# A routed feed-forward stage on one core: Gelu moved to PSUM, result sums moved forward

## What is computed

```python
x = x + xattn(layernorm(x), ctx, ...)          # 32 batches x 128 tokens x 128, 16 heads, 77 keys
# the stage that the change touches: 8 experts, the best 2 for each token
n = layernorm(x)
top_v, top_i = top_k(gate_scores(n), 2);  gate_probs = softmax(top_v)
h   = gelu(einsum('bsd,edf->ebsf', n, W1) + b1)   # F = 512
eo  = einsum('ebsf,efd->ebsd', h, W2) + b2
out = x + sum of the two chosen eo, each times its gate_prob
```

## Time and profile before

| | us |
|---|---|
| median of 3 runs | 387.59 (386.9 to 391.44) |
| the profiled execution, its own time | 386.44 |
| its span | 384.7 |
| busy PE, DVE, ACT, POOL | 341.3, 304.0, 291.5, 276.7 |
| mean granted clock of PE | 0.966 |

### The profile page before, as it was taken

How to read it: one execution, slowest core, us unless ns; L and a number is a source line. 1 busy time by engine, 2 the same in 40 slices (tenths; PEclk the granted TensorE clock), 3 DMA queues, 4 the chain that set the end, 5 groups by cost and what they waited for, 6 DMA issues and landing times.

```text
span 384.7 us, 14132 instructions
## 1 busy us (share of the span) xinstructions
PE 341.3 (89%) x3564; PEld 290.9 (76%) x3565; DVE 304.0 (79%) x972; ACT 291.5 (76%) x846; POOL 276.7 (72%) x493
## 2 busy tenths in 40 slices
PE   4799999999999999999997689999999999999800
PEld 3467777777777777777775579999999999999700
DVE  6678999999999999999998647676665666668773
ACT  3799999999999999999986465666566666666621
POOL 5632487777877777777744647888989888789873
PEclk9999999999999999999999869999999999999965
DMA  3132023321333011210000221223222223259156
GB/s 91 44 81 78 23 79 100 100 67 62 97 97 88 33 40 43 85 36 22 23 29 18 64 65 50 65 66 84 73 83 73 69 69 82 56 152 284 33 147 180
DMA packets 42570, 29.19 MB, mean 76 GB/s; under 512 B 5443, under 2 KB 39311, under 8 KB 42528
## 3 DMA queue, kind: packets, MB, share of 16 engines
q1 hardware_dynamic: 34848, 18.60, 18.2%
q0 software_dynamic: 4320, 8.53, 6.6%
q10 hardware_dynamic: 3360, 1.57, 1.4%
HBM read 17.53 MB, written 11.62 MB: 76 GB/s over the span
## 4 chain that ended last, share of the span: by engine, by line
PE 57%; DVE 21%; issue 9%; DMA 4%; ACT 3%; POOL 2%; DVEq 2%; ACTq 0%; SPq 0%; POOLq 0%
PE ps_s L912 15%; PE ps_s L923 13%; PE ps_t L635 7%; PE ps_o L646 4%; PE ps_s L619 4%; DVE sums L1217 3%; DVE mx L1200 3%; PE ps_s L609 3%; DVE rows L1285 2%; PE ps_t L905 2%; PE ps_x L666 1%; DVE pr L1210 1%; DMA ys<-results 1%; PE ps_o L660 1%; DVE x L1239 1%
## 5 line engine op out<-in xcount | busy, mean ns | idle before, releaser
L567 POOL DMA_INDIRECT results<-eo,didx x71 | 70.8, 997 | 22.1 <-POOL didx L556 10.0
L452 POOL DMA_INDIRECT lists<-rows,slots x64 | 66.7, 1043 | 17.7 <-issue 16.9
L912 PE MATMUL ps_s<-xtT,w1c 128*128 128x128 f32 x568 | 78.3, 282 | 1.1 <-DVE xtT L1623 1.0
L923 PE MATMUL ps_s<-w2s,hT 128*128 x568 | 75.8, 277 | 0.2 <-ACT hT L1148 0.2
L963 ACT ACTIVATE pT<-ps_t 77x512 f32<-77x512 f32 x128 | 73.9, 595 | 2.0 <-PE ps_t L635 2.0
L635 PE MATMUL ps_t<-identf,pr 128*77 128x128 f32 x512 | 72.8, 275 | 0.8 <-ACT pT L963 0.7
L912 PEld LDWEIGHTS ps_s<-xtT,w1c 128*128 128x128 f32 x568 | 71.5, 198 | 2.0 <-DVE xtT L1623 1.9
L1144 ACT ACTIVATE w1c<-w1s 128x512 f32 x71 | 44.8, 631 | 35.4 <-PE ps_s L912 34.2
L923 PEld LDWEIGHTS ps_s<-w2s,hT 128*128 128x128 f32 x568 | 69.7, 193 | 0.5 <-issue 0.4
L1637 DVE TENSOR_TENSOR h<-ps_s,b1T 128x512 f32<-128x512 f32 x71 | 49.0, 690 | 25.5 <-PE ps_s L912 23.8
L635 PEld LDWEIGHTS ps_t<-identf,pr 128*77 128x77 f32 x512 | 58.6, 147 | 6.9 <-issue 4.6
(11 more groups left out here) (211 smaller groups left out, 609.3 us busy)
## 6 DMA issues: line engine op xcount, KB each, us to landing
xt<-lists SPq DMA_DIRECT2D x71, 66.0 KB
ys<-results SPq DMA_DIRECT2D x14, 256.0 KB, 3.7
xin<-in_x_dram SPq DMA_DIRECT2D x16, 128.0 KB
w1s<-in_L_ffn_W_dram SPq DMA_DIRECT2D x8, 256.0 KB, 3.2
w2s<-in_L_ffn_W_dram SPq DMA_DIRECT2D x8, 256.0 KB, 3.5
out_dram<-x SPq DMA_DIRECT2D x5, 256.0 KB, 5.6
cin<-in_ctx_dram SPq DMA_DIRECT2D x16, 77.0 KB
results<-eo,didx POOLq DMA_INDIRECT x71
```

What stands on the lines that cost most here:

```text
L452: nc.gpsimd.indirect_dma_start(lists, bass.IndirectOffsetOnAxis(ap=slots[:, r, s * TOPK + k:s * TOPK + k + 1], axis=0), rows[:, r, s, k, : ...
L567: nc.gpsimd.indirect_dma_start(results, bass.IndirectOffsetOnAxis(ap=didx[:, r:r + 1], axis=0), eo[:, r, :], None, bounds_check=TOPK * NTO ...
L912: last = nc.tensor.matmul(ps_s[:, r, c * P:(c + 1) * P], w1c[:, r, c * P:(c + 1) * P], xtT[:, r, :], start=True, stop=True)
L923: last = nc.tensor.matmul(ps_s[:, 2 + r, 0:D], hT[:, r, c * P:(c + 1) * P], w2s[:, bass.ds(e + c * D, D)], start=(c == 0), stop=(c == FC - 1))
```

## The change

- Bias and Gelu become one operation of ACT, straight from PSUM: 4 activations of 128x128, each with the bias column of its 128 features. DVE's `h` goes, and with it the buffer `h`, `h_ready`, `tab_b` and `bias_at`. PE's up product of j+1 now waits for `act_ready` of j-1.
- ACT's step j has another order: Gelu of j first, then the weights of j+2. ACT reads `tab_w` twice in a step.
- 17 batches (`SUMMED`) are summed on DVE beside tiles 60 to 70, one or two for each tile, and 7 more right behind the last tile. POOL and ACT share in the last 8 batches alone. `chances(0, ...)` moves from steps 0 to 2 to step 60.
- SP issues the stores of chunks 0 to 3 before the late loads. Of chunks 6 and 7, SP loads the first results and ACT the second ones. ACT issues the last store.
- POOL's last tile doesn't wait for `pace`, and the last three tiles write none.

```diff
-    EARLY = 11
-    LATER = 3
+    SUMMED = (2, 2, 1, 2, 1, 2, 1, 2, 1, 2, 1)
+    SUMS_FROM = N_TILES - len(SUMMED)
...
-            return b >= EARLY and b % 8 in POOL_OF_8
+            return b >= PART and b % 8 in POOL_OF_8
...
+        def late_results(eng, k):
+            all_returned(eng, N_TILES)
+            for c in range(PART // CH, NB // CH):
                 eng.dma_start(ys[:, c, k, :, :], res[c, k]).then_inc(y_loaded[c], 16)
...
-            all_returned(sp, N_TILES)
-            load_results(sp, PART // CH)
-
-            for c in range(LATER, NB // CH):
+            for c in range(sum(SUMMED) // CH):
+                store(sp, c)
+            late_results(sp, 0)
+            for c in range(sum(SUMMED) // CH, NB // CH - 1):
                 store(sp, c)
...
-                after_tile(pool, FE["paced"], j - 2)
+                if not known(j) or j < N_TILES - 1:
+                    after_tile(pool, FE["paced"], j - 2)
...
-                nc.gpsimd.memset(pace[:, m % 2, :], 0.0).then_inc(FE["paced"], 1)
+                if not known(j) or j < N_TILES - 3:
+                    nc.gpsimd.memset(pace[:, m % 2, :], 0.0).then_inc(FE["paced"], 1)
...
-                    after_tile(pe, FE["h_ready"], j - 1)
+                    after_tile(pe, FE["act_ready"], j - 1)
...
             def tile(j, m):
                 r = m % 2
+                if has(j, 0, N_TILES):
+                    e = act.value_load(tab_w[0:1, j:j + 1] if known(j) else tab_w[0:1, bass.ds(j, 1)],
+                                       min_val=0, max_val=(NE - 1) * F)
+                    after_tile(act, FE["up_done"], j)
+                    after_tile(act, FE["down_done"], j - 2)
+                    settled(act)
+                    for c in range(FC):
+                        last = nc.scalar.activation(hT[:, r, c * P:(c + 1) * P], ps_s[:, r, c * P:(c + 1) * P], ACT.Gelu,
+                                                    bias=b1T[:, bass.ds(e // P + c, 1)])
+                    last.then_inc(FE["act_ready"], 1)
                 if has(j, 2, N_TILES):
...
-                if has(j, 0, N_TILES):
-                    after_tile(act, FE["h_ready"], j)
-                    after_tile(act, FE["down_done"], j - 2)
-                    nc.scalar.activation(hT[:, r, :], h[:, r, :], ACT.Gelu).then_inc(FE["act_ready"], 1)
...
-            act.wait_ge(p_step, 3)
-            for c in range(PART // CH):
-                weigh(c)
-            all_returned(act, N_TILES)
-            for c in range(PART // CH + 1, NB // CH):
-                load_results(act, c)
-            for c in range(LATER):
-                store(act, c)
+            late_results(act, 1)
             act.wait_ge(p_step, 6)
             for c in range(PART // CH, NB // CH):
                 weigh(c)
+            store(act, NB // CH - 1)
...
+            def sum_batches(a, z):
+                if a == 0:
+                    for stage in range(3):
+                        chances(0, stage)
+                    dve.wait_ge(p_step, 3)
+                for b in range(a, z):
+                    if b % CH == 0:
+                        after_y(dve, b // CH)
+                    first_sum(b)
+                for b in range(a, z):
+                    second_sum(b)
...
-                if has(j, 2, N_TILES):
-                    r = m % 2
-                    after_tile(dve, FE["act_ready"], j)
-                    after_tile(dve, FE["up_done"], j + 2)
-                    nc.vector.tensor_tensor(h[:, r, :].rearrange("p (c t) -> p c t", c=FC),
-                                            ps_s[:, r, :].rearrange("p (c t) -> p c t", c=FC),
-                                            b1T[:, bass.ds(e1, FC)].unsqueeze(2).to_broadcast([P, FC, P]), ALU.add
-                                            ).then_inc(FE["h_ready"], 1)
+                if known(j) and SUMS_FROM <= j < N_TILES:
+                    sum_batches(sum(SUMMED[:j - SUMS_FROM]), sum(SUMMED[:j - SUMS_FROM + 1]))
...
-            dve.wait_ge(all_given, 1)
-            second_sum(EARLY - 1)
-            for c in range(EARLY // CH, NB // CH):
-                mine = [b for b in range(c * CH, (c + 1) * CH) if b >= EARLY and not on_pool(b)]
+            sum_batches(sum(SUMMED), PART)
+            for stage in range(3):
+                chances(1, stage)
+            dve.wait_ge(p_step, 6)
+            for c in range(PART // CH, NB // CH):
+                mine = [b for b in range(c * CH, (c + 1) * CH) if not on_pool(b)]
```

More of the change, by code:

```diff
@@ L56, in xattn_moe_kernel @@
     N_ZEROS = 3
-    AHEAD = 3
     AFTER = 3
@@ L64, in xattn_moe_kernel @@
     PTT = 64
-    EARLY = 11
-    LATER = 3
+    SUMMED = (2, 2, 1, 2, 1, 2, 1, 2, 1, 2, 1)
+    SUMS_FROM = N_TILES - len(SUMMED)
     POOL_OF_8 = (2, 5, 7)
-    assert NB % 4 == 0 and PART % 4 == 0 and max(PART_TILES) + AHEAD <= PTT
+    assert NB % 4 == 0 and PART % 4 == 0 and max(PART_TILES) <= PTT
     assert HG * SK <= 512 and HG == 4
-    TT = N_TILES + AHEAD
+    TT = N_TILES
     assert (NE - 1) * FC < 32
@@ L583, in _ @@
             steps(pool, give_back, 0, N_TILES - 1, LOOPED, N_TILES - 2, FRING, between)
-            pool.nop(nofuse=True).then_inc(all_given, 1)
-            for c in range(NB // CH):
+            for c in range(PART // CH, NB // CH):
                 mine = [b for b in range(c * CH, (c + 1) * CH) if on_pool(b)]
@@ L894, in _ @@
             steps(pe, step, 1, 17, 5, 14)
-            pe.wait_ge(tab_ready, 3)
+            pe.wait_ge(tab_ready, 1)
             pe.wait_ge(l_ffn, 16 * FFN_LOADS)
@@ L943, in between @@
                 elif j == LOOPED:
-                    pe.wait_ge(tab_ready, 5)
+                    pe.wait_ge(tab_ready, 2)
             steps(pe, tile, -2, N_TILES, LOOPED, N_TILES - 3, FRING, between)
@@ L1155, in between @@
                 elif j == LOOPED:
-                    act.wait_ge(tab_ready, 5)
+                    act.wait_ge(tab_ready, 2)
             steps(act, tile, -2, N_TILES - 1, LOOPED, N_TILES - 3, FRING, between)
@@ L1451, in table_rows @@
                                         ).then_inc(skip_ready, 1)
[L1452 to L1457, removed]
+                nc.vector.tensor_copy(tab_w[:, a:z], tabs[part][0][0:1, 0:z - a]).then_inc(tab_ready, 1)
             def counted():
@@ L1579, in _ @@
             steps(dve, step, 0, 18, 6, 13)
-            dve.wait_ge(tab_ready, 3)
+            dve.wait_ge(tab_ready, 1)
             dve.wait_ge(wpt_copied, 2)
@@ L1605, in second_sum @@
                                                ALU.mult, ALU.add).then_inc(sum2, 1)
-            def tile(j, m):
[L1608 to L1612, removed]
+            def sum_batches(a, z):
[9 more added lines that the diff above has]
+                    second_sum(b)
+            def tile(j, m):
                 if has(j, -1, N_TILES):
-                    q = (m - 1) % FRING
+                    q, t = (m - 1) % FRING, j - 1
+                    e = dve.value_load(tab_w[0:1, t:t + 1] if known(t) else tab_w[0:1, bass.ds(t, 1)],
+                                       min_val=0, max_val=(NE - 1) * F)
+                    e2 = e // FC
                     after_dma(dve, returned, j - 1 - FRING, q)
@@ L1645, in between @@
                     second_norm(NP - 1, NP - 1)
-                elif 0 <= j < 3:
-                    chances(0, j)
                 elif j == 3:
@@ L1667, in between @@
                 elif j == LOOPED:
-                    dve.wait_ge(tab_ready, 5)
-            steps(dve, tile, -3, N_TILES, LOOPED, N_TILES - EARLY - 1, FRING, between)
+                    dve.wait_ge(tab_ready, 2)
+            steps(dve, tile, -3, N_TILES, LOOPED, SUMS_FROM - 1, FRING, between)
+            sum_batches(sum(SUMMED), PART)
             for stage in range(3):
                 chances(1, stage)
-            dve.wait_ge(all_given, 1)
-            second_sum(EARLY - 1)
-            for c in range(EARLY // CH, NB // CH):
-                mine = [b for b in range(c * CH, (c + 1) * CH) if b >= EARLY and not on_pool(b)]
+            dve.wait_ge(p_step, 6)
+            for c in range(PART // CH, NB // CH):
+                mine = [b for b in range(c * CH, (c + 1) * CH) if not on_pool(b)]
                 after_y(dve, c)
```

26 lines of the change are left out of this document (6 added, 20 removed).

## The result

The changed kernel takes 400.12 us (median of 4, 397.0 to 401.67), the kernel before 389.51 beside it (median of 4, 386.9 to 391.59). The ratio is 1.0266, with 95% between 1.0164 and 1.0367: some 10 us slower. The profiled execution of the changed kernel took 401.67, its span is 399.9.

A forecast was written before the change was run, and what follows sets the result against it. PE bound the steady tiles at 1.90 us; Gelu before copy makes 2.05. 228.2 + 68 x 2.05 + 0.5 + 0.5 = 368.6 to the last Gelu; with the end, span 388.9 (+4.2), time 390.7 us, range 380.5 to 402.

The forecast's parts named there:

- rival 2: ACT in the steady tile: reads hidden, but register work for four bias addresses longer; 2.12 to 2.22 us, 395 to 402; chance 0.13.
- What bounds the kernel: Steady feed-forward tiles: PE always busy, 1.90 us a tile; with Gelu before the weights' copy, ACT may make PE wait.
- The steady tile: Loop from up product of j to that of j+2: PE waits 0.25 to 0.34 us per two tiles; 2.05 a tile.
- PE's end to the first Gelu: Steady loop: 0.16 us from the end of PE's work to ACT's start, taken from the old copy's start.
- ACT's sequencer: ACT's step, two table reads: reads lie beside ACT's work; the sequencer's own round is 2.0 us, just under 2.05.
- What would show it: Signs at 300 to 320: PE's windows fall from 20.0 to about 18.5 busy, up products 2.05 us apart.
- The first tiles: Start of feed-forward: removing `h` keeps about 1 us of PE's 1.76 idle; tile 2's Gelu at 228.2, from 229.22.
- cost nothing beside the tiles: DVE's sums beside the late tiles: up to two batches, 4 x 0.26 us, replace 0.69 for `h`; no cost.
- The last tile to the end: Behind the last Gelu: `eo` 1.85, loads 4.5, POOL's sums 3.85 after landing, DRAIN's end 6.2 later; span 388.9.
- Rival 1: ACT's sequencer isn't ahead of ACT, so reads aren't hidden: 2.37 us a tile, 22 us more, 412; chance 0.12.
- Rival 3: Steady tile: PE stays the bound at about 1.90 us, 10.2 us less, 380.5; chance 0.13.
- Rival 4: End of the kernel doesn't shorten: loads no faster, a chunk holds DVE, or DRAIN grows; +3, 394; chance 0.07.

The follow-up runs named there:

- the repeat: The changed kernel run once more, unchanged, in a later group of runs: 400.1 us, 1.0245 of the kernel before.
- One read: The changed kernel with ACT reading its table once, the Gelus taking expert 0's bias columns from fixed addresses (wrong biases): 393.26 us, 1.006 of before.
- copy first: The changed kernel with ACT's old order: copy of the weights of j+2, then the four Gelus of j: 390.81 us, 1.0016 of before.
- Gelu's table early: The changed kernel with a single-column Gelu on ACT ahead of the first tile, to load the table early: 398.31 us, 1.0214 of before.
- the best kernel: The changed kernel with weights copied first, one packed table read, no POOL behind the last scatter, DVE's read before sums, early Gelu table: 381.81 us, 0.9775 of before.
- Stores behind the loads: The changed kernel with SP waiting for the late loads before it issues the stores of chunks 4 to 6: 401.28 us, 1.026 of before.
- Before, with no POOL at the end: The kernel before with all batches behind the last tile summed on DVE, none on POOL or ACT: 400.98 us, 0.9921 of before.
- the second group: Follow-up runs testing repairs, on one chip and sharing executions of the kernel before, which took 404.41 us there.
- the first group: Follow-up runs testing which part of the change costs time and why, sharing executions of the kernel before, which took 390.25 us there.

## Why the prediction was right in the range and short in size

The forecast was 390.7 from a base of 386.44, that is +4.3 us. The time is +10.6. It lies inside the range, in the case that got 0.13 (rival 2). The forecast's "within 2%" is wrong: the repeat has 1.0211 as its lower end.

The 6.4 us that the forecast lacks, by the landmarks of the table: 143.81 - 140.4 = 3.4 between the Gelus of tiles 2 and 70, 21.38 - 18.85 = 2.5 behind the last Gelu's end, 0.6 in the first tiles, -0.1 in the last Gelu. Another 3.1 is the base, 389.51 in place of 386.44, and 390.7 + 6.4 + 3.1 = 400.2 is the time. So the range held in part by luck: rival 2's sum has neither the end nor the base in it.

**What bounds the kernel, and the order of ACT's step: right.** The Gelu waits for the down product of j-2 and the copy for the Gelu, as foretold. Taking back the order gave 0.15 us in a tile, as much as the forecast's 2.05 - 1.90; with the read gone, the new order alone costs 2.01 - 1.90 = 0.11.

**The steady tile, 2.05: mis-sized.** Term by term for two tiles, forecast against the table above: four Gelus 1.08 to 1.17, measured 1.13. Copy and PE's start 0.75, measured 0.74. Up and down product 2.06, measured 0.99 + 1.16 = 2.15. PE's end to the first Gelu 0.16, measured 0.25 (0.20 to 0.23 in most tiles, up to 0.68 in single ones). The last two are the terms that were too small, by 0.09 each. The wait before the Gelu was taken from the copy of before, behind one read; the new Gelus stand behind a read, four computed addresses and the waits of `up_done` and `down_done`. The step "ACT's sequencer" treated its round as a bound of its own, 2.0 "just under 2.05", that costs nothing as long as it is the shorter one. But part of it lies behind the moment at which PE ends, 0.25 us with the read and 0.09 without it, and adds to the loop, whatever the length of the round. "One read" measures what read and addresses cost: 0.12 us a tile, and 136.3 us in place of 143.8 between the Gelus of tiles 2 and 70. And the round itself, 1.93 to 1.98 in "copy first", was as estimated. PE's 0.09 is measured but not tested.

For one Gelu the Trainium skill, "ScalarE: Activation LUTs", section "What ACT_TABLE_LOAD costs", gives 280 ns + 0.833 ns for each column and an overlap of 93 ns. For 128 columns that is an estimate of 387 ns, with starts 0.294 us apart. The trace has 369 ns on the mean, and four in 1.14 us, which is (1.14 - 0.37) / 3 = 0.26 apart. By that page four hold ACT for 4 x 0.294 = 1.18 us until the copy, and 1.13 was measured: from PSUM it is a little cheaper here, and this isn't what was missed.

**What would show it: one wrong sign.** PE's windows were to fall to 18.5 busy. PE's row stayed at 19.99; the weight loads fell to 18.84 and the count by 11%. The ends of matmuls are modelled, so a short wait for weights hides in a matmul's length.

**The first tiles, -1.0: -0.42.** PE's turn of the last rows did follow the first up product at once (225.89, with no idle time). What came next is the table load and four Gelus ahead of the copy for tile 2. The forecast saw the table load there, and priced the gain at what was left. "Gelu's table early" shows that moving the load is worth 2.2 us, more than the removal of `h`. Up product 2 stood 0.70 us idle for its weights, and the clock of 0.50, which the forecast took as the same both ways, lasted beyond 232.

**The last tile to the end.** From the last Gelu's end to DRAIN's end it was 21.81 us before, 388.7 - 369.85 = 18.85 foretold, 21.38 measured. The new end gained 0.4 us, not 3.0. Term by term:
- `eo`: 1.85 foretold, 380.97 + 0.29 - 378.28 = 2.98 measured. DVE's read of the table for the last `eo` stands in its order behind `second_sum`'s wait. The down product had ended at 379.57. The sequencer at that line, reading twice and late:

```profile
L1616 DVEq TENSOR_LOAD <-tab_w x2: 306/408/510, 378.0 to 379.9; - x2
```

   This is a queue that was moved past without being priced: sums "cost nothing beside the tiles", but their waits hold the reads behind them. So `eo` starts 1.40 behind the down product's end, before it was 0.28. In the best kernel, with the read ahead, it starts 0.60 behind it (365.28 to 365.88), and two of DVE's sums (365.23 and 365.62) still stand before it. The read's place is worth 0.8 of the 1.1 us, and 0.3 is left for the sums themselves.
- POOL's scatter 0.2 behind `eo`: 0.81. The same scatter was 2.18 behind it before, so most of that delay was POOL's own queue, but 0.67 of idle time that no engine ended remains.
- Loads landed after 4.5: chunk 7 after 5.97, though four stores were gone from there. "Stores behind the loads" takes 0.4 off. What slows them stays open: each chunk now comes by two queues, and a kernel that loads each chunk by one wasn't run.
- From there to POOL's last sum 3.85: 3.04. DRAIN 6.2 behind it: 6.2, as foretold, and it ended the span.

**The base.** The sum was made against an execution of 386.44. With 390.3 as the median of before in later runs, the same steps give 394.6. A beginning that varied by 4.3 us between profiled executions isn't in any range that I gave.

**The rivals.** Rival 1 (2.37 a tile) fell: the mean is 2.13, and PE ended 25.5 of the 27.5 us that ACT stood idle before the Gelus. Rival 2 named 2.12 to 2.22 us a tile and 395 to 402. The tile and the time came out there, the tile by reads and register work in series with PE and not as a round of their own, the time with help from the end and the base. Rival 3 fell (1.90). Rival 4 was right about the end, which didn't shorten: it and the tile together make the difference.

## What to carry to other kernels

When an operation is moved between two waits of a closed loop, count what its engine's sequencer does between the wait and the start (table reads, computed addresses). A round of the sequencer that is shorter than the loop isn't free, if part of it lies behind the event that the loop waits for. The same holds for an engine's other work: sums put ahead of the last `eo` held it up. Keep the copy that feeds the bound engine ahead of the work that waits for that engine, and read what the next step needs before a wait, not behind it.

## What the runs showed of the hardware

- POOL's closing DRAIN takes 7.0 to 7.6 us, and 8.75 in "Before, with no POOL at the end". It ended 6.2 us behind POOL's last sum in both kernels, and 402.6 - 396.4 = 6.2 behind the last scatter where POOL had no sums. It costs nothing if POOL ends early: the kernel of before gained 0.8% by it.
- The table load for Gelu takes 1.28 us and the Gelu starts 1.29 behind its start (226.31 to 227.60). The Trainium skill, "ScalarE: Activation LUTs", section "What ACT_TABLE_LOAD costs", counts a drain of 1.38 us more for each switch. No such time shows here, where ACT had been idle for 5.27 us.
- Beside the second group the kernel before took 404.41 us, beside the others 390.3. The steady tile isn't what is longer (1.94 for 1.90). Some 6 us are in the attention part, from ACT's first to its last `recT`: 192.8 to 194.1 us in the four traces of that group, 186.6 to 187.8 in the ten others. The cause isn't known; the first group, with the same chip number, doesn't show it. Ratios of the same edit can be compared across groups only with their intervals, of up to 1% each way.
